# Surface flow: one wide DMA sums the K and H terms and the squares, and u is updated a slot later

## The chip, the core and the metric

The kernel runs on one core of a Trainium2 chip. The metric is the device time of one execution in microseconds (us), the median over the runs. All times are of this core. The engines are PE (TensorE, matmuls), DVE (VectorE), ACT (ScalarE), POOL (GpSimd, which here only issues DMAs that add) and SP (SyncE, which issues plain DMAs).

## What is computed

The input x is 4 x 16 images of 512 x 512 in fp32. Four layers follow each other: a window attention with an MLP (layer 0), a surface flow (layer 1), and two convolution pairs with relu (layers 2 and 3). The change lies in layer 1, which runs ten steps on each of the 64 images:

```
def step(u, _):
    ux, uy, uxx, uxy, uyy = _derivs(u)      # 3x3 Sobel filters, each result clipped to -10..10
    g2 = ux * ux + uy * uy
    denK = jnp.maximum(1.0 + g2, EPS)
    K = jnp.clip((uxx * uyy - uxy * uxy) / (denK * denK + EPS), -5.0, 5.0)
    denH = jnp.sqrt(1.0 + g2 + EPS)
    H = ((1.0 + uy * uy) * uxx - 2.0 * ux * uy * uxy + (1.0 + ux * ux) * uyy) / (2.0 * denH ** 3 + EPS)
    H = jnp.clip(H, -5.0, 5.0)
    diff = jnp.clip(alpha * K + beta * H, -1.0, 1.0)
    u = u + DT * diff
    u = jnp.pad(u[:, :, 1:-1, 1:-1], ((0, 0), (0, 0), (1, 1), (1, 1)), mode='edge')
    return (u, None)
```

## The kernel before

**Units and slots.** The surface flow holds a group of 8 images in SBUF (`surf_u`) and runs all ten steps on it, then stores it and loads the next; there are 8 groups. A group is cut into 17 units: each is 64 + 64 partitions with 2 x 512 columns, with 2 rows of halo. Group, step and unit make 8 x 10 x 17 = 1360 units, which go through a pipeline that is written out by hand: in slot `s` each engine does its share for units `s`, `s-1`, ... in a fixed order (`slot(s, par)` of each engine, called by `every_slot`). Buffers in `surf_deriv` and `surf_rest` exist twice, by the parity of the unit. `R_FIELDS` names the fields of `surf_rest` in their order in memory; each is 1024 fp32 numbers (4096 bytes) in each of 128 partitions.

**What a unit goes through.** PE makes the derivatives (L927 from u, L932 from `surf_deriv`, and the sum of the three H terms from `surf_rest`). ACT copies them from PSUM (L986, L990), squares q, p and B in one instruction (L1003), and makes 1/denK^2 and 1/denH^3 by logarithms and exponentials (L1007, L1016, L1019, L1021 give rH; L1026, L1028, L1030 give rK). DVE clips the derivatives (L1106, L1093, L1088), makes m (L1116), multiplies K together (L1124), Ha and Hc from the squares q2 and p2 (L1132), mB and nK (L1136), H (L1148), clips K and H (both on L1099), and clips their sum into `surf_ds`, scaled (L1154).

**The sums by DMA.** POOL issues DMAs that add their source to what the destination holds. In slot `s` they are, in this order: rH += rK of unit `s-4` (L1043), which is alpha K + beta H; q2 += p2 of unit `s-2` (L1049), which is g2; nK += B2 of unit `s-2` (L1054); and two that add `surf_ds` of unit `s-4` to `surf_u` (L1060), crosswise between the halves of the partitions. The waits ahead of the two sums that matter:

```
pool.wait_ge(k_clipped, s - 3)
pool.wait_ge(h_clipped, s - 3)
...
pool.wait_ge(squared, s - 1)
pool.wait_ge(hac_done, s - 1)
```

`hac_done` is told by L1132, which reads q2 and p2. DVE's L1154 waits for the sum of L1043 (`ds_sum`), ACT's L1007 for that of L1049 (`g_sum`).

**After the update.** One slot on, DVE writes the edge columns of u (L1141) and tells `updated`. SP waits for it, and exchanges halo rows between units at the end of a step (L817 to L837), or stores the group and loads the next at the end of a group (L804, L631). `unit_ready` then lets PE take the unit in its next step, 17 slots after the last one.

Of the kernel before, what the change touches and what calls it, by code (L numbers as in the profile page):

```python
# [11 lines left out]
ALU = mybir.AluOpType  # L12
# [630 lines left out]
def surface_stage(nc, x1, u10, mats, alpha_in, beta_in, STEPS, units, u, moved):  # L643
# [26 lines left out]
    with ExitStack() as ctx:  # L670
# [3 lines left out]
        def sem(name):  # L674
            return ctx.enter_context(nc.semaphore(name))
# [8 lines left out]


        D_FIELDS = ["m", "q0", "q1", "p0", "p1", "B0", "B1", "A0", "A1", "C0", "C1"]
        R_FIELDS = ["q20", "q21", "p20", "p21", "B20", "B21", "Ha0", "Ha1", "Hc0", "Hc1", "mB0", "mB1",
                    "nK0", "nK1", "rK0", "rK1", "rH0", "rH1"]
        deriv = sb("surf_deriv", [P, len(D_FIELDS), TW + 2])
        rest = sb("surf_rest", [P, len(R_FIELDS), TW])  # L690
        ds = sb("surf_ds", [P, 2, W + 4])
# [6 lines left out]
        clipped_pb, clipped_q, clipped_ac, taken_ac = sem("clipped_pb"), sem("clipped_q"), sem("clipped_ac"), sem("taken_ac")  # L698
        squared, m_done, hac_done, mbnk_done = (
            sem(n) for n in ("squared", "m_done", "hac_done", "mbnk_done"))  # L700
        g_sum, nk_sum, ds_sum, u_added = sem("g_sum"), sem("nk_sum"), sem("ds_sum"), sem("u_added")
        g_ln, g_pow, pow_ln, rh_done, den_squared, den_ln, rk_done = (
            sem(n) for n in ("g_ln", "g_pow", "pow_ln", "rh_done", "den_squared", "den_ln", "rk_done"))
        k_made, k_clipped, h_made, h_clipped, ds_clipped = (
# [3 lines left out]
        def wait(eng, s, value):  # L708

            if not isinstance(value, int) or value > 0:  # L710
                eng.wait_ge(s, value)

        def here(unit):

            return not isinstance(unit, int) or 0 <= unit < TOTAL
# [6 lines left out]
        def field(name, par=0, rows=slice(0, P), lo=0, n=TW):  # L722

            i, t, pad = place(name, par)
            return t[rows, i, pad + lo:pad + lo + n]

        def pair(a, pa, b, pb, lo=0, n=TW):

            (i, t, pad), (j, _, _) = place(a, pa), place(b, pb)
            return t[:, i:j + 1:j - i, pad + lo:pad + lo + n]  # L730

        def triple(a, b, c, par):

# [243 lines left out]
        @block.scalar  # L977
        def _(act):

            act.preload_act_table_set("natural_log_exp_and_others")  # L980

            def copy(par, phase, crossed, straight, lo=0):

                if crossed and straight:
                    n = TW - lo
                    return act.activation(pair(*crossed, *straight, lo, n), made_both(par, phase, lo, n), ACT.Copy)  # L986
                side, f = (CROSS, crossed) if crossed else (DIAG, straight)
                if lo:
                    return act.activation(field(*f, lo=lo, n=W), made_in(par, phase)[:, bank(par, phase, side, 1), :], ACT.Copy)
                return act.activation(field(*f), made_side(par, phase, side), ACT.Copy)  # L990

            def slot(s, par):

                o = 1 - par
                if here(s - 1) or here(s - 2):
                    act.wait_ge(made_ac, s)
                    wait(act, mbnk_done, s - 2)
                    copy(o, 2, ("A", o) if here(s - 1) else None, ("C", par) if here(s - 2) else None, by_dve(par)).then_inc(copied_ac, 1)
                if here(s - 2):
                    act.wait_ge(clipped_q, s - 1)  # L1000
                    act.wait_ge(clipped_pb, s)
                    wait(act, nk_sum, (s - 3) * 16)
                    act.activation(triple("q2", "p2", "B2", par), triple("q", "p", "B", par), ACT.Square).then_inc(squared, 1)  # L1003
                if here(s - 3):
                    act.wait_ge(g_sum, (s - 2) * 16)
                    wait(act, ds_clipped, s - 4)
                    act.activation(field("rH", o), field("q2", o), ACT.Ln, bias=1.0 + EPS).then_inc(g_ln, 1)  # L1007
                if here(s) or here(s - 1):
                    act.wait_ge(made_pb, s + 1)
                    if here(s - 2):  # L1010
                        wait(act, squared, s - 1)
                    wait(act, m_done, min(s - 1, TOTAL) if isinstance(s, int) else s - 1)
                    copy(par, 0, ("p", par) if here(s) else None, ("B", o) if here(s - 1) else None).then_inc(copied_pb, 1)
                if here(s - 3):
                    act.wait_ge(g_ln, s - 2)
                    act.activation(field("rH", o), field("rH", o), ACT.Exp, scale=1.5).then_inc(g_pow, 1)  # L1016
                if here(s - 3):
                    act.wait_ge(g_pow, s - 2)
                    act.activation(field("rH", o), field("rH", o), ACT.Ln, bias=EPS, scale=2.0).then_inc(pow_ln, 1)  # L1019
                    act.wait_ge(pow_ln, s - 2)  # L1020
                    act.activation(field("rH", o), field("rH", o), ACT.Exp, scale=-1.0).then_inc(rh_done, 1)  # L1021
                if here(s):
                    act.wait_ge(made_qn, s + 1)
                    copy(par, 1, ("q", par), None).then_inc(copied_q, 1)
                if here(s - 3):
                    act.activation(field("rK", o), field("q2", o), ACT.Square, bias=1.0).then_inc(den_squared, 1)  # L1026
                    act.wait_ge(den_squared, s - 2)
                    act.activation(field("rK", o), field("rK", o), ACT.Ln, bias=EPS).then_inc(den_ln, 1)  # L1028
                    act.wait_ge(den_ln, s - 2)
                    act.activation(field("rK", o), field("rK", o), ACT.Exp, scale=-1.0).then_inc(rk_done, 1)  # L1030

            every_slot(slot, act, TOTAL + 3)

        @block.gpsimd
        def _(pool):
            def slot(s, par):

                if here(s - 4):
                    pool.wait_ge(k_clipped, s - 3)
                    pool.wait_ge(h_clipped, s - 3)  # L1040
                    wait(pool, ds_sum, (s - 4) * 16)
                    pool.sem_inc(sums_begun, 1)
                    pool.dma_start(field("rH", par), field("rK", par), accum_op=ALU.add).then_inc(ds_sum, 16)  # L1043
                if here(s - 2):
                    pool.wait_ge(squared, s - 1)
                    pool.wait_ge(hac_done, s - 1)
                    wait(pool, g_sum, (s - 2) * 16)
                    pool.sem_inc(sums_begun, 1)
                    pool.dma_start(field("q2", par), field("p2", par), accum_op=ALU.add).then_inc(g_sum, 16)  # L1049
                    pool.wait_ge(mbnk_done, s - 1)  # L1050
                    pool.wait_ge(squared, s - 1)
                    wait(pool, nk_sum, (s - 2) * 16)
                    pool.sem_inc(sums_begun, 1)
                    pool.dma_start(field("nK", par), field("B2", par), accum_op=ALU.add).then_inc(nk_sum, 16)  # L1054
                if here(s - 4):
                    pool.wait_ge(ds_clipped, s - 3)
                    wait(pool, u_added, (s - 4) * 32)
                    k = bass.ds((s - 4) % UNITS, 1)
                    for found, rows in CROSSED:
                        pool.dma_start(u[rows, k, :, :].rearrange("p a t w -> p (a t w)"), flat(ds[found, :, :]),  # L1060
                                       accum_op=ALU.add).then_inc(u_added, 16)

            every_slot(slot, pool, TOTAL + 4)

        @block.vector
        def _(dve):
# [34 lines left out]
            def slot(s, par):  # L1101

                o = 1 - par
                if here(s - 2):
                    dve.wait_ge(made_ac, s)
                    dve.tensor_scalar(field("q", par), field("q", par), *CLIP).then_inc(clipped_q, 1)  # L1106
# [21 lines left out]
                if here(s - 2):  # L1128
# [6 lines left out]
                    dve.wait_ge(clipped_pb, s)  # L1135
                    dve.scalar_tensor_tensor(out=pair("mB", par, "nK", par), in0=pair("m", 0, "A", par), scalar=-1.0,  # L1136
                                             in1=pair("B", par, "C", par), op0=ALU.mult, op1=ALU.mult).then_inc(mbnk_done, 1)
                if here(s - 5):
                    dve.wait_ge(u_added, (s - 4) * 32)
                    uv = u[:, bass.ds((s - 5) % UNITS, 1), :, 2:W + 2].rearrange("p a t w -> p (a t) w")  # L1140
                    dve.tensor_scalar(uv[:, :, 0:W:W - 1], uv[:, :, 1:W - 1:W - 3], 1.0, None, ALU.mult).then_inc(updated, 1)  # L1141
                if here(s) or here(s - 1):
                    dve.wait_ge(copied_pb, s + 1)
# [1 line left out]
                if here(s - 3):  # L1145
# [3 lines left out]
                                             in1=field("rH", o), op0=ALU.mult, op1=ALU.mult).then_inc(h_made, 1)  # L1149
                    dve.wait_ge(h_made, s - 2)  # L1150
                    clip_to(field("rH", o), 1).then_inc(h_clipped, 1)
                if here(s - 4):
                    dve.wait_ge(ds_sum, (s - 3) * 16)
                    dve.tensor_scalar(ds[:, :, 2:W + 2], field("rH", par).rearrange("p (t w) -> p t w", t=2), DT, -DT,  # L1154
                                      ALU.min, ALU.max).then_inc(ds_clipped, 1)

            every_slot(slot, dve, TOTAL + 5)


PAIRS_A_GROUP = 4  # L1160
# [381 lines left out]
```

## Time and profile before

| What | Value |
|---|---|
| Median of 3 runs | 26456.31 us (26447.13 to 26471.87) |
| Profiled execution, its own time | 26429.67 us |
| Its span in the trace | 26427.9 us |
| Granted clock of TensorE, mean | 0.989 |
| PE busy | 25368.3 us (96%) |
| DVE busy | 22784.0 us (86%) |
| ACT busy | 22108.6 us (84%) |
| POOL busy | 5842.9 us (22%) |
| DMA queue of POOL (q0) | 2858.13 MB, 59.7% of 16 engines' span |

The span is that of the program's instructions on the core; the execution's own time is 2 us longer. Busy shares are means over all stages: attention up to about 5300 us, the surface flow to about 24500 us, the convolutions to the end. Only the middle one is touched. In the tables of the trace, "L1132" is line 1132 of the kernel before, an arrow names the releaser of an idle time, and `out<-in` are the program's tensors.

### The profile page before, as it was taken

The numbers are of one execution on the slowest core, as the hardware profiler recorded it, in microseconds if no ns is written. First come the engines' busy times: TensorE is split into PE (matmuls) and PEld (weight loads), VectorE is DVE, ScalarE is ACT, GpSimd is POOL, SyncE is SP. The second block draws the span as 40 slices with busy tenths as digits, with TensorE's granted clock in tenths as the row PEclk, the third lists the DMA queues.
The fourth block names the chain that finished last, engine by engine and source line by source line (L and its number), as shares of the span: only waits on it lengthen the run. The fifth ranks groups of instructions, "written<-read, shape, count | busy, mean of one in ns | idle before, by whom it ended". The sixth has DMA issues, their size and how long they took to land. (4 is left out here: it accounts for less than half of the span.)

```text
span 26427.9 us, 783402 instructions
## 1 busy us (share of the span) xinstructions
PE 25368.3 (96%) x323352; PEld 12659.5 (48%) x323352; DVE 22784.0 (86%) x22077; ACT 22108.6 (84%) x19199; POOL 5842.9 (22%) x6804
## 2 busy tenths in 40 slices
PE   8999999899999999999999999999999999999799
PEld 5666666544444443444444345434534444444465
DVE  6666666699999999999999999999999999999322
ACT  6666666699999999999999899999999998999111
POOL 0000000023323332333233233323323332333000
PEclk9999999999999999999999999999999999999899
DMA  1111111288888888888888888888888888888765
GB/s 33 32 32 32 32 32 32 44 149 156 154 171 156 154 156 170 156 155 166 159 156 154 168 155 156 158 166 156 155 167 158 156 155 167 155 156 158 120 117 101
DMA packets 1550407, 3439.19 MB, mean 130 GB/s; under 512 B 547441, under 2 KB 679153, under 8 KB 1546481
## 3 DMA queue, kind: packets, MB, share of 16 engines
q0 software_dynamic: 805120, 2858.13, 59.7%
q1 hardware_dynamic: 742512, 536.63, 10.3%
q8 instruction: 2649, 43.40, 0.7%
q14 instruction: 126, 1.02, 0.0%
HBM read 294.21 MB, written 201.33 MB: 19 GB/s over the span
## 5 line engine op out<-in xcount | busy, mean ns | idle before, releaser
L927 PE MATMUL surf_ps<-surf_u,surf_matf 64*64 64x512 f32 x87040 | 18838.6, 591 | 364.3 <-DVE surf_rest L1148 152.2
L927 PEld LDWEIGHTS surf_ps<-surf_u,surf_matf 64*64 64x64 f32 x87040 | 7290.0, 133 | 10802.3 <-issue 10547.6
L932 PE MATMUL surf_ps<-surf_deriv,surf_matf 64*64 64x512 f32 x54400 | 12051.9, 593 | 0.0
L932 PE MATMUL surf_ps<-surf_rest,surf_matf 64*64 64x512 f32 x32640 | 7237.1, 590 | 4.6 <-DVE surf_rest L1136 2.7
L1003 ACT ACTIVATE surf_rest<-surf_deriv 128x3072 f32<-128x3072 f32 x1360 | 3766.7, 2770 | 478.0 <-DVE surf_deriv L1106 394.8
L986 ACT ACTIVATE surf_deriv<-surf_ps 128x2048 f32<-128x2048 f32 (+1 forms) x2718 | 3901.0, 1435 | 258.1 <-PE surf_ps L932 251.1
L932 PEld LDWEIGHTS surf_ps<-surf_deriv,surf_matf 64*64 64x64 f32 x54400 | 3723.2, 133 | 40.8 <-issue 29.9
L1060 POOL DMA_DIRECT2D surf_u<-surf_ds x2720 | 2273.3, 973 | 4814.3 <-DVE surf_ds L1154 4314.9
L1132 DVE SCALAR_TENSOR_TENSOR surf_rest<-surf_rest,surf_deriv 128x2048 f32<-128x2048 f32 x1360 | 3106.3, 2284 | 0.3
L1136 DVE SCALAR_TENSOR_TENSOR surf_rest<-surf_deriv 128x2048 f32<-128x2048 f32 x1360 | 3106.1, 2284 | 0.0
L1049 POOL DMA_DIRECT2D surf_rest<-surf_rest x1360 | 1162.6, 855 | 7177.1 <-DVE surf_rest L1132 7166.1
L1088 DVE TENSOR_SCALAR surf_deriv<-surf_deriv 128x1024 f32<-128x1024 f32 (+1 forms) x2722 | 2597.6, 954 | 123.5 <-ACT surf_deriv L986 117.5
L1043 POOL DMA_DIRECT2D surf_rest<-surf_rest x1360 | 1218.8, 896 | 5033.6 <-DVE surf_rest L1099 5033.1
L932 PEld LDWEIGHTS surf_ps<-surf_rest,surf_matf 64*64 64x64 f32 x32640 | 2282.5, 133 | 37.3 <-issue 30.2
L1099 DVE TENSOR_SCALAR surf_rest<-surf_rest,surf_clips 128x1024 f32<-128x1024 f32 x2720 | 2209.3, 812 | 99.3
L1148 DVE SCALAR_TENSOR_TENSOR surf_rest<-surf_ps,surf_dt_ab,surf_rest 128x1024 f32<-128x1024 f32 x1360 | 1736.7, 1277 | 37.3 <-PE surf_ps L932 37.0
L1124 DVE SCALAR_TENSOR_TENSOR surf_rest<-surf_rest,surf_dt_ab 128x1024 f32<-128x1024 f32 x1360 | 1735.7, 1276 | 0.0
L407 ACT ACTIVATE att_hid<-att_w,att_b_fc 128x2048 f32<-128x2048 f32 x256 | 503.7, 1967 | 1465.0 <-PE att_w L278 1465.0
L1093 DVE TENSOR_SCALAR surf_deriv<-surf_ps 128x1024 f32<-128x1024 f32 x1359 | 1654.9, 1218 | 0.0
L1116 DVE SCALAR_TENSOR_TENSOR surf_deriv<-surf_deriv 128x1024 f32<-128x1024 f32 x1360 | 1654.7, 1217 | 0.0
L486 DVE TENSOR_REDUCE att_mx<-att_w 128x32 f32<-128x2048 f32 x512 | 1173.1, 2291 | 519.9 <-PE att_w L207 519.9
L472 DVE SCALAR_TENSOR_TENSOR att_acc<-att_xin,att_vec,att_acc 128x512 f32<-128x512 f32 x2048 | 1534.6, 749 | 54.3
(105 smaller groups left out, 31999.3 us busy)
## 6 DMA issues: line engine op xcount, KB each, us to landing
surf_rest<-surf_rest POOLq DMA_DIRECT2D x4080, 512.0 KB, 5.9
surf_u<-surf_ds POOLq DMA_DIRECT2D x2720, 258.0 KB, 5.0
att_xin<-in_x SPq DMA_DIRECT2D x2048, 41.2 KB, 2.1
attended<-att_out_rows SPq DMA_DIRECT2D x1024, 64.0 KB, 2.0
surf_u<-attended SPq DMA_DIRECT2D x512, 128.0 KB
chain_us<-flowed SPq DMA_DIRECT2D x512, 128.0 KB, 3.8
chain_xs<-attended SPq DMA_DIRECT2D x512, 128.0 KB, 4.7
out<-chain_outs SPq DMA_DIRECT2D x504, 128.0 KB, 2.8
```

Source lines behind the costliest of these rows:

```text
L927: mm = pe.matmul(dst[out, bank(par, phase, CROSS, t), :], matf[rows, mat, :], u[rows, k, t, off + 2:off + 2 + W], start=(i == 0), stop=(i ...
L932: mm = pe.matmul(dst[out, bank(par, phase, DIAG, t), :], matf[rows, mat, :], field(*fields[i], rows=rows, lo=t * W + off, n=W), start=(i = ...
L986: return act.activation(pair(*crossed, *straight, lo, n), made_both(par, phase, lo, n), ACT.Copy)
L1003: act.activation(triple("q2", "p2", "B2", par), triple("q", "p", "B", par), ACT.Square).then_inc(squared, 1)
L1060: pool.dma_start(u[rows, k, :, :].rearrange("p a t w -> p (a t w)"), flat(ds[found, :, :]), accum_op=ALU.add).then_inc(u_added, 16)
L1088: return dve.tensor_scalar(both, both, *CLIP)
L1093: return dve.tensor_scalar(pair(*first, *second, 0, W), made_both(par, phase, 0, W), *CLIP)
L1099: return dve.tensor_scalar(f, f, clips[:, which, 0:1], clips[:, which, 1:2], ALU.min, ALU.max)
L1124: dve.scalar_tensor_tensor(out=field("rK", par), in0=field("nK", par), scalar=minus_alpha, in1=field("rK", par), op0=ALU.mult, op1=ALU.mul ...
L1132: dve.scalar_tensor_tensor(out=pair("Ha", par, "Hc", par), in0=pair("q2", par, "p2", par), scalar=1.0, in1=pair("A", par, "C", par), op0=A ...
L1136: dve.scalar_tensor_tensor(out=pair("mB", par, "nK", par), in0=pair("m", 0, "A", par), scalar=-1.0, in1=pair("B", par, "C", par), op0=ALU. ...
L1148: dve.scalar_tensor_tensor(out=field("rH", o), in0=made_side(par, 1, DIAG), scalar=beta, in1=field("rH", o), op0=ALU.mult, op1=ALU.mult).t ...
```

## The change

The order of the fields in `surf_rest` is changed so that rH lies next to q2 and rK next to p2 of the same parity. One DMA with rows of 2 fields (8192 bytes) then does rH += rK of unit `s-4` and q2 += p2 of unit `s-2` at once. It waits for what either of the two waited for. The semaphores `g_sum` and `ds_sum` become one, `summed`. DVE's clip of the sum into `surf_ds`, the two DMAs that add it to u, and the edge columns are written one slot later, the first two at the start of the slot's code.

```diff
-        R_FIELDS = ["q20", "q21", "p20", "p21", "B20", "B21", "Ha0", "Ha1", "Hc0", "Hc1", "mB0", "mB1",
-                    "nK0", "nK1", "rK0", "rK1", "rH0", "rH1"]
+        R_FIELDS = ["rH0", "q20", "rK0", "p20", "Ha0", "B20", "rH1", "q21", "rK1", "p21", "Ha1", "B21",
+                    "Hc0", "Hc1", "mB0", "mB1", "nK0", "nK1"]
...
+        def run_of(a, b, par):
+
+            (i, t, pad), (j, _, _) = place(a, par), place(b, par)
+            return t[:, i:j + 1, :].rearrange("p f w -> p (f w)")
...
                 if here(s - 3):
-                    act.wait_ge(g_sum, (s - 2) * 16)
+                    act.wait_ge(summed, (s - 2) * 16)
                     wait(act, ds_clipped, s - 4)
...
-                if here(s - 4):
-                    pool.wait_ge(k_clipped, s - 3)
-                    pool.wait_ge(h_clipped, s - 3)
-                    wait(pool, ds_sum, (s - 4) * 16)
+                if here(s - 5):
+                    pool.wait_ge(ds_clipped, s - 4)
+                    wait(pool, u_added, (s - 5) * 32)
+                    k = bass.ds((s - 5) % UNITS, 1)
+                    for found, rows in CROSSED:
+                        pool.dma_start(u[rows, k, :, :].rearrange("p a t w -> p (a t w)"), flat(ds[found, :, :]),
+                                       accum_op=ALU.add).then_inc(u_added, 16)
+                if here(s - 2) or here(s - 4):
+                    if here(s - 4):
+                        pool.wait_ge(k_clipped, s - 3)
+                        pool.wait_ge(h_clipped, s - 3)
+                    if here(s - 2):
+                        pool.wait_ge(squared, s - 1)
+                        pool.wait_ge(hac_done, s - 1)
+                    wait(pool, summed, (s - 2) * 16)
                     pool.sem_inc(sums_begun, 1)
-                    pool.dma_start(field("rH", par), field("rK", par), accum_op=ALU.add).then_inc(ds_sum, 16)
+                    first, last = 0 if here(s - 4) else 1, 1 if here(s - 2) else 0
+                    pool.dma_start(run_of(("rH", "q2")[first], ("rH", "q2")[last], par),
+                                   run_of(("rK", "p2")[first], ("rK", "p2")[last], par), accum_op=ALU.add).then_inc(summed, 16)
...
+                if here(s - 5):
+                    dve.wait_ge(summed, (s - 2) * 16)
+                    wait(dve, u_added, (s - 5) * 32)
+                    dve.tensor_scalar(ds[:, :, 2:W + 2], field("rH", o).rearrange("p (t w) -> p t w", t=2), DT, -DT,
+                                      ALU.min, ALU.max).then_inc(ds_clipped, 1)
                 if here(s - 2):
                     dve.wait_ge(made_ac, s)
...
-                if here(s - 5):
-                    dve.wait_ge(u_added, (s - 4) * 32)
-                    uv = u[:, bass.ds((s - 5) % UNITS, 1), :, 2:W + 2].rearrange("p a t w -> p (a t) w")
+                if here(s - 6):
+                    dve.wait_ge(u_added, (s - 5) * 32)
+                    uv = u[:, bass.ds((s - 6) % UNITS, 1), :, 2:W + 2].rearrange("p a t w -> p (a t) w")
...
-                if here(s - 4):
-                    dve.wait_ge(ds_sum, (s - 3) * 16)
-                    dve.tensor_scalar(ds[:, :, 2:W + 2], field("rH", par).rearrange("p (t w) -> p t w", t=2), DT, -DT,
-                                      ALU.min, ALU.max).then_inc(ds_clipped, 1)
```

What stands on POOL in one slot of the loop, before. The `L711` row ahead of L1049 waits for `squared` and `hac_done`, the one ahead of L1060 for `ds_clipped`, and the one at the top for both clips, K's and H's:

```order
L711 REGISTER_ALU
L1043 DMA surf_rest<-surf_rest 128x1024
L711 REGISTER_ALU
L1049 DMA surf_rest<-surf_rest 128x1024
L1054 DMA surf_rest<-surf_rest 128x1024
L711 REGISTER_ALU
L1060 ISA
L1060 DMA surf_u<-surf_ds 64x1032
L1060 ISA
L1060 DMA surf_u<-surf_ds 64x1032
```

And after, for one slot of the same loop, where `L1048` are the additions to u, `L1060` is the wide sum and `L1067` that of nK. The `L711` row ahead of L1048 waits for `ds_clipped`, the one ahead of L1060 for `squared`, `hac_done`, `k_clipped` and `h_clipped`:

```order
L711 REGISTER_ALU
L1048 ISA
L1048 DMA surf_u<-surf_ds 64x1032
L1048 ISA
L1048 DMA surf_u<-surf_ds 64x1032
L711 REGISTER_ALU
L1060 DMA surf_rest<-surf_rest 128x2048
L1067 DMA surf_rest<-surf_rest 128x1024
```

The sum of rH and rK has moved behind `squared` and `hac_done`; the additions to u, which stood behind the nK sum of the slot before, still stand there.

DVE, before, from the second half of one slot in the loop into the next one:

```order
L1148 SCALAR_TENSOR_TENSOR surf_rest<-surf_ps,surf_dt_ab,surf_rest 128x1024
L1099 TENSOR_SCALAR surf_rest<-surf_rest,surf_clips 128x1024
L1154 TENSOR_SCALAR surf_ds<-surf_rest 128x2x512
L1106 TENSOR_SCALAR surf_deriv<-surf_deriv 128x1024
L1093 TENSOR_SCALAR surf_deriv<-surf_ps 128x2x512
L1116 SCALAR_TENSOR_TENSOR surf_deriv<-surf_deriv 128x1024
```

And after, at the same place, where L1159 answers to L1148, L1105 to L1099, L1113 to L1154, L1117 to L1106, L1099 to L1093, and L1127 to L1116:

```order
L1159 SCALAR_TENSOR_TENSOR surf_rest<-surf_ps,surf_dt_ab,surf_rest 128x1024
L1105 TENSOR_SCALAR surf_rest<-surf_rest,surf_clips 128x1024
L1111 REGISTER_ALU
L711 ISA
L1113 TENSOR_SCALAR surf_ds<-surf_rest 128x2x512
L1117 TENSOR_SCALAR surf_deriv<-surf_deriv 128x1024
L1099 TENSOR_SCALAR surf_deriv<-surf_ps 128x2x512
L1127 SCALAR_TENSOR_TENSOR surf_deriv<-surf_deriv 128x1024
```

The clip into `surf_ds` has gone from the end of one slot's code to the start of the next one's, and stands between the same two neighbours as before.

## Rows read from the trace of the kernel before

**Rows 1.** Windows: stretch, then busy us (count) of PE, PEld, DVE, ACT, POOL; clock, DMA share, GB/s.
```profile
15000.00:20000.00 5000.00, 4909.09 (x45340) 2162.54 (x45336) 4852.91 (x4600) 4759.03 (x3895) 1518.75 (x1767) 0.99 0.86 160
```

**Rows 2.** Line L1154, whole span: duration ns min/median/max, first and last start us.
```profile
L1154 DVE TENSOR_SCALAR surf_ds<-surf_rest x1360: 683/687/697, 5336.4 to 24518.4; 128x1024 f32<-128x1024 f32 x195
```

**Rows 3.** Timeline of SP's queue, 11740 to 12300 us: start, duration, line.
```profile
12008.46 0.61 SPq L825 DMA_DIRECT2D surf_u<-surf_u  x1
...
12021.31 1.27 SPq L837 DMA_DIRECT2D surf_u<-surf_u  x1
...
12242.54 0.61 SPq L825 DMA_DIRECT2D surf_u<-surf_u  x1
```

**Rows 4.** Waits, 5100 to 23900 us: total us, times, longest us.
```profile
DVE surf_u L1141 <- DMA surf_u<-surf_ds: 191.9, 95, 6.2
PE surf_ps L927 <- DVE surf_rest L1148: 140.2, 83, 4.9
PE surf_ps L927 <- SPq L898: 132.9, 8, 25.8
...
DVE surf_ds L1154 <- DMA surf_rest<-surf_rest: 31.2, 26, 3.9
```

**Rows 5.** Timeline of DVE, one undisturbed slot: start us, duration us.
```profile
12025.28 0.69 DVE L1154 TENSOR_SCALAR surf_ds<-surf_rest 128x1024 f32<-128x1024 f32 x1
...
12030.67 0.81 DVE L1099 TENSOR_SCALAR surf_rest<-surf_rest,surf_clips 128x1024 f32<-128x1024 f32 x1
12031.40 2.28 DVE L1132 SCALAR_TENSOR_TENSOR surf_rest<-surf_rest,surf_deriv 128x2048 f32<-128x2048 f32 x1
...
12037.01 1.28 DVE L1148 SCALAR_TENSOR_TENSOR surf_rest<-surf_ps,surf_dt_ab,surf_rest 128x1024 f32<-128x1024 f32 x1
...
12039.05 0.69 DVE L1154 TENSOR_SCALAR surf_ds<-surf_rest 128x1024 f32<-128x1024 f32 x1
```

**Rows 6.** Timeline of POOL, the same slot; in brackets idle before and releaser.
```profile
12026.70 1.65 POOL L1060 DMA_DIRECT2D surf_u<-surf_ds  x2 [3.13 <-DVE surf_ds L1154]
12032.16 0.90 POOL L1043 DMA_DIRECT2D surf_rest<-surf_rest  x1 [3.81 <-DVE surf_rest L1099]
12034.42 0.86 POOL L1049 DMA_DIRECT2D surf_rest<-surf_rest  x1 [1.37 <-DVE surf_rest L1132]
12036.49 0.86 POOL L1054 DMA_DIRECT2D surf_rest<-surf_rest  x1 [1.20 <-DVE surf_rest L1136]
```

**Rows 7.** Lines L1043, L1049, L1054, from 8000 to 20000 us: issue to landing.
```profile
L1043 POOL DMA_DIRECT2D surf_rest<-surf_rest x849: 892/896/922, 8004.0 to 19986.8; - x170
...
DMA to landing us min/median/max: 4.5/5.1/12.4
...
L1049 POOL DMA_DIRECT2D surf_rest<-surf_rest x849: 850/852/885, 8006.3 to 19989.0; - x170
...
DMA to landing us min/median/max: 5.1/5.6/13.4
...
L1054 POOL DMA_DIRECT2D surf_rest<-surf_rest x849: 854/857/1759, 8008.4 to 19991.1; - x170
...
DMA to landing us min/median/max: 5.8/7.0/15.9
```

**Rows 8.** DMA queues, 8000 to 20000 us: packets, MB, share of 16 engines.
```profile
q0 software_dynamic: 502756, 1784.73, 82.2%
```

**Rows 9.** Line L1043 at the end of a group, 9900 to 10235 us.
```profile
L1043 POOL DMA_DIRECT2D surf_rest<-surf_rest x20: 892/897/899, 9912.5 to 10220.7; - x20
...
DMA to landing us min/median/max: 5.0/7.6/11.0
```

**Rows 10.** Page, DMA issues: count, KB each, median us to landing.
```profile
surf_u<-surf_ds POOLq DMA_DIRECT2D x2720, 258.0 KB, 5.0
```

**Rows 11.** Timeline of ACT, the slot of rows 5.
```profile
12026.68 2.77 ACT L1003 ACTIVATE surf_rest<-surf_deriv 128x3072 f32<-128x3072 f32 x1 [0.28 <-DVE surf_deriv L1106]
...
12034.24 1.06 ACT L1021 ACTIVATE surf_rest<-surf_rest 128x1024 f32<-128x1024 f32 x1
```

More of the change, by code:

```diff
@@ L700, in surface_stage @@
             sem(n) for n in ("squared", "m_done", "hac_done", "mbnk_done"))
-        g_sum, nk_sum, ds_sum, u_added = sem("g_sum"), sem("nk_sum"), sem("ds_sum"), sem("u_added")
+        summed, nk_sum, u_added = sem("summed"), sem("nk_sum"), sem("u_added")
         g_ln, g_pow, pow_ln, rh_done, den_squared, den_ln, rk_done = (
@@ L1036, in slot @@
             def slot(s, par):
-                if here(s - 4):
-                    pool.wait_ge(k_clipped, s - 3)
-                    pool.wait_ge(h_clipped, s - 3)
-                    wait(pool, ds_sum, (s - 4) * 16)
+                if here(s - 5):
[13 more added lines that the diff above has]
+                    wait(pool, summed, (s - 2) * 16)
                     pool.sem_inc(sums_begun, 1)
-                    pool.dma_start(field("rH", par), field("rK", par), accum_op=ALU.add).then_inc(ds_sum, 16)
+                    first, last = 0 if here(s - 4) else 1, 1 if here(s - 2) else 0
+                    pool.dma_start(run_of(("rH", "q2")[first], ("rH", "q2")[last], par),
+                                   run_of(("rK", "p2")[first], ("rK", "p2")[last], par), accum_op=ALU.add).then_inc(summed, 16)
                 if here(s - 2):
[L1045 to L1049, printed above, removed]
                     pool.wait_ge(mbnk_done, s - 1)
@@ L1054, in slot @@
                     pool.dma_start(field("nK", par), field("B2", par), accum_op=ALU.add).then_inc(nk_sum, 16)
-                if here(s - 4):
[L1056 to L1063, printed above, removed]
+            every_slot(slot, pool, TOTAL + 5)
         @block.vector
@@ L1151, in slot @@
                     clip_to(field("rH", o), 1).then_inc(h_clipped, 1)
-                if here(s - 4):
-                    dve.wait_ge(ds_sum, (s - 3) * 16)
-                    dve.tensor_scalar(ds[:, :, 2:W + 2], field("rH", par).rearrange("p (t w) -> p t w", t=2), DT, -DT,
-                                      ALU.min, ALU.max).then_inc(ds_clipped, 1)
-            every_slot(slot, dve, TOTAL + 5)
+            every_slot(slot, dve, TOTAL + 6)
 PAIRS_A_GROUP = 4
```

## The prediction

> **What bounds the kernel now.** I read the windows of the surface flow first. In 5000 us of it PE is busy 4909, DVE 4853 and ACT 4759, at a granted clock of 0.99, and the DMA engines 0.86 of the time [rows 1]. PE has the least slack, and three others stand right behind it. DVE does its last clip (L1154) 1360 times between 5336.4 and 24518.4 us [rows 2]: 19182 / 1359 = 14.11 us a slot on average. The undisturbed slot is shorter: SP's first exchange transfer of a step (L825) starts at 12008.46 and again at 12242.54, 234.08 us for 17 slots, or 13.77 us [rows 3]. That is PE's own pace; the difference comes from moves at the ends of groups and a few waits. PE's named waits over the whole stage are small: 140.2 us for DVE's L1148 and 132.9 us for SP; DVE waits 191.9 us for the additions to u [rows 4]. So nothing that the change could shorten is worth more than some 1% of the time. What it could lengthen is a loop through DVE and a DMA, so the timeline of DVE and of POOL and the landing times decide.
>
> **What the change really moves.** The label says "one slot later", but the rows of the order show less. DVE's clip into ds stood last in a slot, right before the next slot's L1106 (the clip of q); now it stands first in a slot, right before that same clip of q. On POOL the additions to u likewise stand where they stood, between the nK sum and the next slot's first sum. What moved is the K+H sum: it was issued as soon as both clips were done, and is now part of a DMA that waits for DVE's L1132 too. Truly one slot later are only DVE's edge columns (L1141) and what SP does behind them.
>
> **The new loop.** Before, DVE's order in a slot is L1154, five other operations, L1099, L1132, L1136, L1141, L1088, L1148, L1099, L1154. The first L1099, the K clip, starts 12030.67 and lasts 0.81; POOL starts the sum 12032.16 (0.68 us behind its end); DVE comes to L1154 at 12039.05 [rows 5, 6]. So 6.89 us lie between issue and use, and the sum lands 5.1 us after its issue at the median and 4.5 at best [rows 7]. It is covered, and DVE waits for it hardly ever (31.2 us in all) [rows 4].
> After, the wide DMA can't be issued before L1132 has ended, since L1132 reads the squares that the DMA overwrites. From that DMA's landing the next clip into ds waits, behind it stand L1106 and all the rest of DVE's slot, up to the next L1132. That closes a loop which no buffer relaxes:
> - From the start of the clip into ds to the end of L1132: 12025.28 to 12031.40 + 2.28 = 8.40 us, back to back [rows 5].
> - From the end of L1132 to POOL's issue: 12034.42 - 12033.68 = 0.74 us [rows 5, 6].
> - From issue to landing of 1024 KB, call it L.
> - From landing to DVE's start: I take none.
>
> The slot is the larger of 13.77 and 9.14 + L. PE stays the bound only if L is at most 4.6 us.
>
> **The price L.** No row shows a DMA of 1024 KB. Two ways lead to it from the rows of 512 KB. First, L1043 lands at best 4.5 us after issue; L1049 is issued 2.26 us behind it (12034.42 - 12032.16) and lands at best 5.1 after issue, so 2.26 + 5.1 - 4.5 = 2.9 us behind it: that is what a second 512 KB costs a queue that is already running [rows 6, 7]. Second, in the 12000 us from 8000 the accumulating queue takes 82.2% of the engines for 1784.73 MB [rows 8]; 0.524 MB then takes 0.524 / 1784.73 x 0.822 x 12000 = 2.9 us of all 16. All rows of that queue are of 4096 or 4128 bytes; no row gives the time of one of 8192, so that bytes are cheaper in wide rows stays a rival. The sum: L = 4.5 + 2.9 = 7.4 at best and 5.1 + 2.9 = 8.0 at the median. One DMA has one fixed part less than two, but that part (4.5 - 2.9 = 1.6 us) was hidden in parallel before, and is in series now.
> The Trainium skill, "DMA: Bandwidth & Descriptors", on the anatomy of one DMA, gives about 2.0 us plus bytes over 436 GB/s, and its rules advise to batch to 1 MiB: by that a second 512 KB adds 1.2 us, L would be 6.3 and the slot 15.4, which is slower too. The rows of this trace show 2.9 us for it, and the sum goes by them.
>
> **The sum.** Undisturbed slot: 9.14 + 8.0 = 17.14 us. At the end of a group SP stores and loads images for some 335 us, and there L1043 lands after 7.6 us at the median, not 5.1 [rows 9]; twice the bytes would meet twice the excess of 2.5, or 5.0; SP also waits between its own batches, and of the 5.0 I take 3.5, so L = 11.5 and the slot 20.7. (With none of it or all of it the total moves by 400 down or 100 up.) Seven such stretches hold 7 x 335 / 20.7 = 113 slots. Stage: 1247 x 17.14 + 113 x 20.7 = 21374 + 2339 = 23713 us. Before it was 19182. The rest of the program (attention ahead, convolutions behind) is not touched; one more drain slot is some 10 us. Profiled execution: span 26427.9, own time 26429.67; plus 4531 plus 10 is 30970. The median of the runs is 27 us above that execution, 0.1%, so I say 31000.
>
> **What else moves, and why I cost it at nothing.** POOL issues three DMAs instead of four plus the same two additions, saving 0.89 us of an engine that has over 9 us idle in a slot [rows 6]. The additions to u are issued at the slot's start, 7 us ahead of the wide DMA, and land in 5.0 us at the median [rows 10], so they aren't in its way. ACT: the squares (L1003) start 1.40 us after the clip into ds (12026.68 - 12025.28) and last 2.77, so they end 2 us before L1132 starts; rh is done (L1021) at 12035.30, before L1148 at 12037.01 [rows 5, 11]. ACT's logarithm needs the same DMA that DVE has by then waited for. The nK sum is used two slots on. The edge columns one slot later: SP's exchange takes 12008.46 to 12022.58 plus a landing [rows 3], and the units it frees are needed more than three slots after the old place of L1141, more than two (over 34 us) after the new one. At a group's end PE waits for SP 132.9 us in all [rows 4]; SP's chain there is made of its own transfers and gets hardly longer, while 17 slots now last 57 us more, so this wait should go. It lies inside the 19182 that I replace.
>
> **Rivals.**
> - Rows of 8192 bytes are cheap, the second half costs 1.2 us or so as the fixed part dominates: slot 9.14 + 6.3 = 15.44, stage 21000, time 28300. For it: one DMA less to complete; against it: both working-outs at 2.9 us. 6%.
> - Rows are free (a packet costs the same at either size): L = 5.1, slot 14.24; stage 19370 plus the groups' ends, say 26900. 2%.
> - The other side: L at most 4.6 us, PE stays the bound, and the waits of DVE for u (191.9) and of PE for L1148 (140.2) go [rows 4]: about 26250. It needs a megabyte to land as fast as the fastest half megabyte. 2%.
> - Worse than forecast: the exchange that L1141 releases starts about 1.6 us after the wide DMA's issue and shares its engines. The nK sum stands at that place now, and lands at 7.0 with 5.8 at best, 1.2 above [rows 7]. With L 1.2 higher in each slot: + 1630, 32600. Or PE, which would now stand idle some 3.4 us in 17, is granted less clock. 8%.
>
> **How the numbers follow.** The forecast has 82%. Its own range: L = 7.4 everywhere gives 16.54 x 1360 = 22494, time 29750; L = 8.9 gives about 32200. I give 29300 to 32200, which leaves out the first three rivals and half of the fourth. Some 0.2% (50 us) is what this measurement can tell from no change; slower by more has 0.96, within it 0.02, faster 0.02.
>
> **What would show it.** DVE's clip into ds waits for "DMA surf_rest<-surf_rest" in nearly each of 1360 slots, about 3.4 us (17.14 - 13.77, plus DVE's old slack of some 0.3), 4700 us in all. The wide DMA lands at a median of 8.0 us. SP's first exchange returns after 291 us, not 234. DVE, ACT and PE fall to about 0.8 of the window, PE waits for DVE's L1148, and the DMA share falls to about 0.7. Wrong if the wide DMA lands much under 7.4, or if ds is clipped without a wait.

## The result, and the profile after

The change makes the kernel slower: 30638.47 us median (30621.95 to 30649.31, 4 runs) against 26459.26 us (26447.13 to 26471.87, 4 runs). The ratio is 1.1579, with a 95% interval of 1.1559 to 1.1599. Forecast was 31000 with 29300 to 32200. The profiled execution took 30633.81 us, its span 30632.0 us; 4204 us more than before's.

The page of the kernel after: busy time by engine, the group of DVE's clip into `surf_ds` (L1113 now; the number behind the last bar is the idle time ahead of it), and the issues of POOL with their KB and median us to landing.

```profile
PE 26643.0 (87%) x323352; PEld 12086.8 (39%) x323352; DVE 22883.3 (75%) x22077; ACT 22162.2 (72%) x19199; POOL 4655.6 (15%) x5446
...
L1113 DVE TENSOR_SCALAR surf_ds<-surf_rest 128x1024 f32<-128x1024 f32 x1360 | 945.9, 696 | 4544.6 <-DMA surf_rest<-surf_rest 4544.5
...
surf_rest<-surf_rest POOLq DMA_DIRECT2D x1358, 1024.0 KB, 7.1
surf_u<-surf_ds POOLq DMA_DIRECT2D x2720, 258.0 KB, 5.0
surf_rest<-surf_rest POOLq DMA_DIRECT2D x1364, 512.0 KB, 8.5
```

DVE does the same work as before (22883 us against 22784), but waits 4544.5 us in one place, where it waited 31.2 [rows 4]. The window that answers to [rows 1]:

```profile
15000.00:20000.00 5000.00, 4300.17 (x37232) 1664.47 (x37224) 4007.19 (x3776) 3917.70 (x3199) 994.49 (x1162) 0.95 0.69 131
```

The row has the same columns as [rows 1]. No engine is full any more, and neither are the DMA engines (0.69, was 0.86). If nobody is full, look for a circle of waits. The waits of the stage (5300 to 28800 us) name its members:

```profile
POOL surf_rest L1060 <- DVE surf_rest L1143: 13488.8, 1344, 5307.1
POOL surf_u L1048 <- DVE surf_ds L1113: 8731.5, 1346, 12.2
DVE surf_ds L1113 <- DMA surf_rest<-surf_rest: 4544.5, 1358, 11.6
ACT surf_rest L1008 <- DVE surf_deriv L1117: 4236.0, 1319, 9.2
PE surf_ps L932 <- issue: 3091.8, 1298, 8.3
```

POOL waits for DVE's L1143 (L1132 before), DVE waits for the DMA that POOL then issues, ACT waits for DVE behind it, and PE, which was the bound, stands idle 3092 us. PE's wait for SP is gone from the list, and DVE's for the additions to u is down to 5.7 us.

The timeline of DVE, three slots on end; from each L1113 to the next is a slot, and L1143 is what POOL waits for.

```profile
15028.59 0.70 DVE L1113 TENSOR_SCALAR surf_ds<-surf_rest 128x1024 f32<-128x1024 f32 x1 [2.48 <-DMA surf_rest<-surf_rest]
...
15044.99 0.69 DVE L1113 TENSOR_SCALAR surf_ds<-surf_rest 128x1024 f32<-128x1024 f32 x1 [2.54 <-DMA surf_rest<-surf_rest]
...
15051.12 2.29 DVE L1143 SCALAR_TENSOR_TENSOR surf_rest<-surf_rest,surf_deriv 128x2048 f32<-128x2048 f32 x1
...
15061.33 0.69 DVE L1113 TENSOR_SCALAR surf_ds<-surf_rest 128x1024 f32<-128x1024 f32 x1 [2.47 <-DMA surf_rest<-surf_rest]
...
15071.85 0.17 DVE L1152 TENSOR_SCALAR surf_u<-surf_u  x1
...
15079.91 0.70 DVE L1113 TENSOR_SCALAR surf_ds<-surf_rest 128x1024 f32<-128x1024 f32 x1 [4.71 <-DMA surf_rest<-surf_rest]
...
15081.11 1.22 DVE L1099 TENSOR_SCALAR surf_deriv<-surf_ps 128x1024 f32<-128x1024 f32 x1
```

And POOL's issues of the wide DMA in the last two of them, and three of SP's L830, the transfer that begins an exchange (L825 before). The first and the last are a step apart, and the second is the next exchange of the same step; a step has four.

```profile
15054.15 0.89 POOL L1060 DMA_DIRECT2D surf_rest<-surf_rest  x1 [6.07 <-DVE surf_rest L1143]
...
15070.56 0.89 POOL L1060 DMA_DIRECT2D surf_rest<-surf_rest  x1 [6.13 <-DVE surf_rest L1143]
```

```profile
15004.41 0.61 SPq L830 DMA_DIRECT2D surf_u<-surf_u  x1
...
15072.05 0.62 SPq L830 DMA_DIRECT2D surf_u<-surf_u  x1
...
15291.93 0.61 SPq L830 DMA_DIRECT2D surf_u<-surf_u  x1
```

The loop can be read off in one slot. DVE's L1113 starts 15044.99; L1143 ends at 15051.12 + 2.29 = 15053.41, which is 8.42 us on. POOL issues 0.74 us later. From 15054.15 to DVE's next L1113 at 15061.33 are 7.18 us. The sum is 16.34 us, where a slot took 13.77 before [rows 3]; undisturbed slots last 16.34 or 16.40 us, by turns, 16.37 on average. The next slot takes 18.58: in it the edge columns (L1152, 15071.85) let SP's exchange go at 15072.05, just 1.5 us behind the wide DMA (15070.56), and DVE waits 4.71 us, not 2.5. SP's period of 17 slots is 15291.93 - 15004.41 = 287.52 us (234.08 before), and over the whole stage:

```profile
L1113 DVE TENSOR_SCALAR surf_ds<-surf_rest x1360: 687/695/700, 5343.9 to 28721.7; 128x1024 f32<-128x1024 f32 x195
...
L1060 POOL DMA_DIRECT2D surf_rest<-surf_rest x1362: 857/892/1279, 5307.5 to 28710.6; - x195
...
DMA to landing us min/median/max: 5.0/7.1/13.5
```

The last start less the first is 23378 us, and 23378 / 1359 = 17.20 us a slot, where [rows 2] gave 14.11. The stage grew by 4196 us: nearly all of the 4204.

The page puts PE's idle time to "issue", that is, to nothing that it can name. The timeline names it. In the slot that begins at 15079.91 PE starts again at 15082.44:

```profile
15082.44 1.12 PE L932 MATMUL surf_ps<-surf_u,surf_matf 64*64 64x512 f32 x2 [4.17 <-issue]
```

That is 0.11 us behind the end of DVE's L1099 (15081.11 + 1.22 = 15082.33), which takes derivatives from PSUM; the code has PE wait for it (`taken_ac`) before it writes there again. Of the 3110 us in idle stretches of PE above 0.3 us in this stage, 3027 us end less than 0.16 us behind an L1099. So PE stands behind DVE, and DVE behind the wide DMA.

### The profile page after: what moved, and what is told of

It is laid out like the page before. It is cut to its first block and busy times, and to the rows that moved or that the text cites. A ratio compares the mean times of both kernels' runs of the same rounds, so it can differ in the third digit from the quotient of the medians.

```text
span 30632.0 us, 780694 instructions
## 1 busy us (share of the span) xinstructions
PE 26643.0 (87%) x323352; PEld 12086.8 (39%) x323352; DVE 22883.3 (75%) x22077; ACT 22162.2 (72%) x19199; POOL 4655.6 (15%) x5446
## 5 line engine op out<-in xcount | busy, mean ns | idle before, releaser
L932 PE MATMUL surf_ps<-surf_u,surf_matf 64*64 64x512 f32 x87040 | 20085.7, 614 | 3278.5 <-issue 3091.8
L932 PEld LDWEIGHTS surf_ps<-surf_u,surf_matf 64*64 64x64 f32 x87040 | 7213.9, 137 | 15623.2 <-issue 15622.2
L937 PE MATMUL surf_ps<-surf_rest,surf_matf 64*64 64x512 f32 x32640 | 8206.1, 654 | 5.8 <-DVE surf_deriv L1101 5.2
L1113 DVE TENSOR_SCALAR surf_ds<-surf_rest 128x1024 f32<-128x1024 f32 x1360 | 945.9, 696 | 4544.6 <-DMA surf_rest<-surf_rest 4544.5
L1048 POOL DMA_DIRECT2D surf_u<-surf_ds x2720 | 2266.7, 980 | 8845.6 <-DVE surf_ds L1113 8731.5
L1060 POOL DMA_DIRECT2D surf_rest<-surf_rest x1362 | 1222.7, 898 | 13609.9 <-DVE surf_rest L1143 13488.8
L1147 DVE SCALAR_TENSOR_TENSOR surf_rest<-surf_deriv 128x2048 f32<-128x2048 f32 x1360 | 3108.1, 2285 | 0.0
L1143 DVE SCALAR_TENSOR_TENSOR surf_rest<-surf_rest,surf_deriv 128x2048 f32<-128x2048 f32 x1360 | 3107.8, 2285 | 0.3
L937 PEld LDWEIGHTS surf_ps<-surf_rest,surf_matf 64*64 64x64 f32 x32640 | 2375.3, 146 | 18.3 <-issue 18.3
L1105 DVE TENSOR_SCALAR surf_rest<-surf_rest,surf_clips 128x1024 f32<-128x1024 f32 x2720 | 2210.6, 813 | 99.6
L1159 DVE SCALAR_TENSOR_TENSOR surf_rest<-surf_ps,surf_dt_ab,surf_rest 128x1024 f32<-128x1024 f32 x1360 | 1738.9, 1279 | 9.1 <-PE surf_ps L937 6.3
L1127 DVE SCALAR_TENSOR_TENSOR surf_deriv<-surf_deriv 128x1024 f32<-128x1024 f32 x1360 | 1656.7, 1218 | 0.0
L1099 DVE TENSOR_SCALAR surf_deriv<-surf_ps 128x1024 f32<-128x1024 f32 x1359 | 1656.4, 1219 | 0.0
```

What stands on the lines that cost most here:

```text
L932: mm = pe.matmul(dst[out, bank(par, phase, CROSS, t), :], matf[rows, mat, :], u[rows, k, t, off + 2:off + 2 + W], start=(i == 0), stop=(i ...
L937: mm = pe.matmul(dst[out, bank(par, phase, DIAG, t), :], matf[rows, mat, :], field(*fields[i], rows=rows, lo=t * W + off, n=W), start=(i = ...
L1105: return dve.tensor_scalar(f, f, clips[:, which, 0:1], clips[:, which, 1:2], ALU.min, ALU.max)
L1127: dve.scalar_tensor_tensor(out=field("m"), in0=field("q", par), scalar=2.0, in1=field("p", par), op0=ALU.mult, op1=ALU.mult).then_inc(m_do ...
L1143: dve.scalar_tensor_tensor(out=pair("Ha", par, "Hc", par), in0=pair("q2", par, "p2", par), scalar=1.0, in1=pair("A", par, "C", par), op0=A ...
L1159: dve.scalar_tensor_tensor(out=field("rH", o), in0=made_side(par, 1, DIAG), scalar=beta, in1=field("rH", o), op0=ALU.mult, op1=ALU.mult).t ...
```

## The experiments

All times are medians, and each ratio is to the kernel before on the same chip. Where a kernel is compared with the kernel after, that is across chips, on which the kernel before took 26459 to 26481 us.

**Two DMAs again, the rest of the change kept.**

```diff
+                if here(s - 4):
+                    pool.wait_ge(k_clipped, s - 3)
+                    pool.wait_ge(h_clipped, s - 3)
+                    wait(pool, ds_sum, (s - 4) * 16)
+                    pool.sem_inc(sums_begun, 1)
+                    pool.dma_start(field("rH", par), field("rK", par), accum_op=ALU.add).then_inc(ds_sum, 16)
+                if here(s - 2):
+                    pool.wait_ge(squared, s - 1)
+                    pool.wait_ge(hac_done, s - 1)
...
-                    dve.wait_ge(summed, (s - 2) * 16)
+                    dve.wait_ge(ds_sum, (s - 4) * 16)
```

> The kernel after, with the wide DMA taken apart into two of 512 KB: rH += rK goes out as soon as both clips are done, q2 += p2 after L1132's counterpart, each with its own semaphore; fields, order of DVE and the update one slot later stay. If the loop from the wide DMA's landing over DVE's clip into ds to its next issue is the cause, DVE's wait ahead of that clip falls from 4544 us to under 100 and the time is that of before, 26250 to 26500; a little less than 26459 if the waits of the edge columns for the additions to u (227 us) go as well. If the later update, or the new order of fields, is the cause, the time stays near 30640.

Measured: 26501.37 us against 26461.26, ratio 1.001 (1.0 to 1.0019). The 4180 us are gone: the wide DMA made them, not the update a slot later. DVE's wait ahead of the clip fell from 4544 to 231 us, not to under 100, and the time came out just above the expected range: the hope of a small gain failed. DVE's wait for the additions to u went (7.3 us), but PE now waits longer for SP at the ends of groups, since SP gets its units a slot later. PE's waits in this kernel:

```profile
PE surf_ps L932 <- SPq L903: 227.1, 13, 28.1
```

Before it was 132.9 us in 8 waits [rows 4].

**The wide DMA alone, all else in its old slot.** It is the kernel before with the new order of fields, `run_of` and the wide DMA of the diff above; DVE keeps its code, with `dve.wait_ge(summed, (s - 1) * 16)` ahead of the clip.

> The kernel before with the new order of fields and the wide DMA, but the clip into ds, the additions to u and the edge columns in the slot where they stood (the nK sum now guarded as in the kernel after). The clip into ds keeps its neighbours on DVE either way, so the loop through the wide DMA is the same: 30640, give or take 200. If the delay of the update by a slot were what costs, it would be near 26460.

Measured: 30469.99 us, ratio 1.151 (1.1492 to 1.1528). The other half of the proof: the wide DMA without the later update costs 4000 us. (In this kernel the nK sum keeps the guard `here(s - 2)` of the kernel after; without it POOL waits at the end for a unit that does not exist, and the kernel never ends.) That it is 170 us below the kernel after is within the 200 that were allowed, but it has a place. DVE's timeline and POOL's in this kernel show where it lies:

```profile
15042.12 0.69 DVE L1160 TENSOR_SCALAR surf_ds<-surf_rest 128x1024 f32<-128x1024 f32 x1 [2.35 <-DMA surf_rest<-surf_rest]
...
15093.51 0.69 DVE L1160 TENSOR_SCALAR surf_ds<-surf_rest 128x1024 f32<-128x1024 f32 x1 [2.36 <-DMA surf_rest<-surf_rest]
...
15109.72 0.69 DVE L1160 TENSOR_SCALAR surf_ds<-surf_rest 128x1024 f32<-128x1024 f32 x1 [2.34 <-DMA surf_rest<-surf_rest]
```

```profile
15035.05 0.89 POOL L1053 DMA_DIRECT2D surf_rest<-surf_rest  x1 [6.06 <-DVE surf_rest L1138]
...
15102.66 0.89 POOL L1053 DMA_DIRECT2D surf_rest<-surf_rest  x1 [6.05 <-DVE surf_rest L1138]
```

Its slot is 16.21 us (15093.51 to 15109.72), and from issue to DVE's clip are 7.06 to 7.07 us, where the kernel after has 7.18. The landing times in the two traces show 7.05 us from issue to landing in undisturbed slots of both, and then 0.12 us from landing to clip in the kernel after, 0.02 in this one. In the kernel after two waits stand ahead of the clip (`summed`, then `u_added`), in this one a single wait. The others go the same way: 0.02 us in the kernel before, which also has one wait, and 0.12 to 0.14 in after_edges_first, wide_rows_4096 and split_late_issue, which have two (ds_before_m, with two, has 0.12 or 0.23). So the second wait fits as the cause of some 0.1 us a slot, 140 of the 170 us, but it was not tried alone.

**The order of fields alone.** R_FIELDS as in the diff, nothing else.

> The kernel before with the new order of fields in surf_rest and nothing else. If memory layout plays no part: 26460 within 30 us. If it does (rows of DVE's and ACT's operands at other distances), the durations of L1132, L1136 and L1003 change and the time with them.

Measured: 26475.84 us, ratio 0.9998 (0.9989 to 1.0007). Layout plays no part; L1132 takes 2285 ns, as before (2284).

**More cover for the DMA: the clip into ds further back on DVE.** In two doses, from the kernel after: the block goes from the start of the slot to a place ahead of the instruction that makes m (ds_before_m), or, unchanged, right behind that instruction (ds_after_m).

```diff
-                if here(s - 5):
-                    dve.wait_ge(summed, (s - 2) * 16)
-                    wait(dve, u_added, (s - 5) * 32)
-                    dve.tensor_scalar(ds[:, :, 2:W + 2], field("rH", o).rearrange("p (t w) -> p t w", t=2), DT, -DT,
-                                      ALU.min, ALU.max).then_inc(ds_clipped, 1)
                 if here(s - 2):
                     dve.wait_ge(made_ac, s)
...
+                if here(s - 5):
+                    dve.wait_ge(summed, (s - 2) * 16)
+                    wait(dve, u_added, (s - 5) * 32)
+                    dve.tensor_scalar(ds[:, :, 2:W + 2], field("rH", o).rearrange("p (t w) -> p t w", t=2), DT, -DT,
+                                      ALU.min, ALU.max).then_inc(ds_clipped, 1)
                 if here(s - 2):
                     dve.wait_ge(clipped_q, s - 1)
                     dve.wait_ge(clipped_pb, s - 1)
```

> The kernel after with the clip into ds moved back by two DVE operations, behind the clip of q and the take from PSUM (0.60 + 1.13 us), so that the DMA has 1.73 us more cover in each slot. Loop: 1360 x 1.73 = 2350 us less than 30638, so 28290. If instead the DMA queue as such is too slow for a slot (contention), or the clock of TensorE is the cause, moving the clip changes little: over 30000.

> The same with the clip one operation further back, behind m: 2.87 us more cover than after. The loop is 16.2 - 2.87 = 13.3 us in undisturbed slots, under the 13.77 of TensorE, so these are as fast as before; slots whose wide DMA lands 2 us late (about a third) still lose some 1.6 us, 0.3 x 1360 x 1.6 = 650: 26600 to 27300. By the rival (contention as such): over 30000.

Measured: 28428.97 us (1.0742, 1.0724 to 1.076) and 27113.48 us (1.0245, 1.0228 to 1.0262). The first dose gives back 2210 / 1360 = 1.6 us a slot for 1.73 us of cover, the second 0.97 more for 1.13, as PE's pace comes near. If the queue as such were too slow, this could not be: all of these kernels move the same bytes. DVE's row of the first:

```profile
15035.82 0.70 DVE L1122 TENSOR_SCALAR surf_ds<-surf_rest 128x1024 f32<-128x1024 f32 x1 [0.73 <-DMA surf_rest<-surf_rest]
```

Its wait of 2.5 us has become 0.73, less by just about the 1.73 us that the clip was moved. The second is still 650 us above the kernel before; m_edges_first below shows what most of that is.

**Late issue without double size.** The kernel split_later with one line more ahead of the sum of K and H; the sum of the squares is issued right behind it.

```diff
+                    wait(pool, hac_done, min(s - 1, TOTAL) if isinstance(s, int) else s - 1)
                     wait(pool, ds_sum, (s - 4) * 16)
```

> The kernel split_later with one more wait: POOL issues the sum of the K and H terms only when L1132's counterpart has ended, as the wide DMA had to, and the sum of the squares right behind it. So the late issue is there, but the clip into ds waits for 512 KB alone (4.5 us at best, 5.4 on average). Loop: 9.14 + 4.6 = 13.74 us at best, just what TensorE takes; landings above that are no longer covered, up to 0.9 us a slot on average: 26700 to 27500. If the late issue alone made the kernel after slow, it would be near 30600; if only the size did, at 26501.

Measured: 27382.19 us, ratio 1.0346 (1.0329 to 1.0364). The late issue by itself costs 920 us over the kernel before (880 over split_later, which differs by the one line), and the second half megabyte in the same DMA takes it to 4180. The waits of this kernel:

```profile
DVE surf_ds L1114 <- DMA surf_rest<-surf_rest: 1036.6, 501, 13.7
```

The wait is there in 501 slots, not in all: its loop is near PE's pace, and mostly the late landings show. Not all of the 920 us need be that wait: ACT's logarithm (L1012) here waits 563 us for the sum of the squares, which is issued later too, where it waited 15.5 us in the kernel before.

**One DMA, rows of 4096 bytes.** The kernel after with the old order of fields, so that rH and q2 lie apart and the one DMA moves two runs a partition.

```diff
-            (i, t, pad), (j, _, _) = place(a, par), place(b, par)
-            return t[:, i:j + 1, :].rearrange("p f w -> p (f w)")
+            if a == b:
+                return field(a, par)
+            return pair(b, par, a, par)
```

> The kernel after, with one DMA for both sums still, but with the old order of fields, so that its rows are two pieces of 4096 bytes that lie apart. Theory: the wide DMA landed 7.1 us after issue where two halves in a row gave 4.5 + 2.9 = 7.4; if the rows of 8192 bytes saved the 0.3 us, this one lands at 7.4 and the time is 1360 x 0.3 = 400 us more, 31040. Rival: the width of rows has no effect and the 0.3 us was a start that two DMAs pay each; then it lands at 7.1 and the time stays 30640. Either way it is far from 26460, since the loop doesn't depend on rows.

Measured: 32331.17 us, ratio 1.2212 (1.2193 to 1.2231), a miss by 1300 us: whether a partition has one run of 8192 bytes or two of 4096 that lie apart matters far more than I had thought. (Width and distance change together here; that the order of fields alone costs nothing was measured with DMAs of 512 KB.) Line L1061 in this kernel, 8000 to 20000 us:

```profile
L1061 POOL DMA_DIRECT2D surf_rest<-surf_rest x650: 1217/1217/2053, 8014.3 to 19996.7; - x163
...
DMA to landing us min/median/max: 7.9/8.0/14.3
```

The issue takes 1.22 us, not 0.89, and the landing 8.0, not 7.1; the 0.9 us are counted from the start of the issue, so the longer issue may be a third of them. 0.9 us a slot is 1220 us of the 1690. The rest is mostly in slots that SP's transfers disturb. Here is one with an exchange, from one clip into ds to the next:

```profile
15060.11 0.70 DVE L1114 TENSOR_SCALAR surf_ds<-surf_rest 128x1024 f32<-128x1024 f32 x1 [3.43 <-DMA surf_rest<-surf_rest]
15081.33 0.69 DVE L1114 TENSOR_SCALAR surf_ds<-surf_rest 128x1024 f32<-128x1024 f32 x1 [7.34 <-DMA surf_rest<-surf_rest]
```

It lasts 21.22 us where the one in the kernel after lasted 18.58.

**SP's exchange out of the wide DMA's way.** The edge columns on DVE right behind the clip into ds; what they wait for has landed by then.

```diff
                                       ALU.min, ALU.max).then_inc(ds_clipped, 1)
+                if here(s - 6):
+                    dve.wait_ge(u_added, (s - 5) * 32)
+                    uv = u[:, bass.ds((s - 6) % UNITS, 1), :, 2:W + 2].rearrange("p a t w -> p (a t) w")
+                    dve.tensor_scalar(uv[:, :, 0:W:W - 1], uv[:, :, 1:W - 1:W - 3], 1.0, None, ALU.mult).then_inc(updated, 1)
...
```

> The kernel after with one move: DVE's edge columns right behind the clip into ds instead of behind L1147, 9 us earlier in the slot. In the kernel after, the wide DMA lands 7.05 us after issue in most slots but at 9.2 in those where SP's exchange, which the edge columns release 1.3 us after the wide DMA's issue, is under way. Theory: the exchange's first big rows collide with the wide DMA; released 9 us earlier they are through by then: some 300 slots lose 2.1 us less, 30638 - 630 = 30000. Rival: SP's ten moves last 14 us and hit a wide DMA wherever they start: 30500 to 30700.

Measured: 30025.65 us, ratio 1.135 (1.1332 to 1.1367): 613 us less from one instruction of 0.17 us moved, as expected. DVE's wait for the wide DMA:

```profile
DVE surf_ds L1113 <- DMA surf_rest<-surf_rest: 3944.3, 1360, 8.5
```

It is 600 us less. Four exchanges a step, nine steps of ten, eight groups are 288 slots; 613 / 288 = 2.1 us each. That is a little too low: the edge columns now stand inside the loop and make its undisturbed slot longer, 16.44 us instead of 16.37. The same move in the kernel with the clip behind m (there the edge columns come first in the slot):

> The kernel with the clip into ds behind m (27113), and the edge columns first in DVE's slot. Theory: what is left over the kernel before, 650 us, is late landings of the wide DMA (DVE waits 892 us for it), of which the exchange causes the greater part: 26500 to 26750. Rival: the 1039 us that ACT's logarithm waits for the clip into ds, which overwrites what it reads, are what is left: 27000 and over.

Measured: 26614.32 us, ratio 1.0063 (1.0048 to 1.0079). 500 of the 650 us that were left go; with cover and with the exchange out of the way the wide DMA is nearly free, but not better than two DMAs.

**A version under both.** Two DMAs, and the edge columns first:

> The kernel split_later (two DMAs of 512 KB, update a slot later, 26501) with the edge columns right behind the clip into ds: their additions have landed long before, so DVE never waits for them, and SP starts only 3.9 us later than in the kernel before instead of 13.8. If the 227 us that TensorE waits for SP in split_later come from the delay, they fall towards 133, and the time to 26300 to 26430, under both kernels. If nothing comes of it, 26460 to 26500.

Measured: 26423.58 us against 26460.37, ratio 0.9988 (0.9979 to 0.9997), the lowest median of all, 37 us under the kernel before. PE's wait for SP:

```profile
PE surf_ps L932 <- SPq L903: 148.5, 7, 29.5
```

The other way, aimed at the same gain, the edge columns of the kernel before moved behind the clip of H, was

> The kernel before with one move: the edge columns behind the clip of H, still in the same slot, 3.3 us later on DVE. If the 227 us that DVE waits there for the additions to u hold up its multiplication of H and then TensorE, these go, and SP starts only 3 us later instead of a slot: 26300 to 26430. If that wait is slack that TensorE's pace hides, no change: 26460. If SP's chain at the ends of groups counts, a few us more.

Measured: 26454.51 us against 26481.15, ratio 0.999 (0.9981 to 0.9999). Both gains are of 0.1%, at the edge of what the runs resolve, and less than hoped; that either kernel is truly faster than the one before is not shown.

## Why the prediction was right

- **What moved.** That the clip into ds keeps its neighbours on DVE and that the sum of K and H is what moves was the key. The two runs that took the change apart bear it out: wide DMA alone 30470, later update alone 26501.
- **The fixed part of the loop.** Forecast 8.40 + 0.74 us; measured 8.42 + 0.74. Right. That DVE would start at once on landing was off by 0.12 us a slot.
- **L, the landing of 1024 KB.** Forecast 8.0 at the median and 7.4 at best; measured 7.1 and, in the undisturbed slots, 7.0. This term was mis-sized, by two things. The second half costs 7.0 - 4.5 = 2.5 us in rows of 8192 bytes, not 2.9. (With rows of 4096 bytes it costs more than 2.9: the DMA lands after 7.9 us at best where the forecast had 7.4. That its median is the forecast 8.0 is luck, two errors of opposite sign.) And I carried over the 0.6 us between best and median of L1043; in the kernel after best and median are 0.1 apart (7.0 and 7.1). I take that 0.6 for traffic of the faster kernel, which is not shown. The rival that rows of 8192 bytes are cheap had a little of the truth: 0.9 us of landing, not the 1.7 that it needed.
- **The disturbed slots.** Forecast: 113 slots at the groups' ends at 20.7 us, which adds 113 x 3.56 = 400 us, and nothing for the exchanges. Measured: 23378 - 1359 x 16.37 = 1130 us over the undisturbed pace, of which the exchange's collision with the wide DMA is at least 613, by experiment. So the exchanges are the term that was wrongly put at nothing. I had named the collision among the worse cases (1.2 us in each slot); it is 2.1 us in one slot of five. The groups' ends cost less than forecast. At one of them:

```profile
L1060 POOL DMA_DIRECT2D surf_rest<-surf_rest x16: 892/895/1274, 13900.7 to 14182.7; - x16
...
DMA to landing us min/median/max: 7.3/8.6/13.1
```

The forecast had 11.5 us there and slots of 20.7; DVE's 14 slots from 13891.50 to 14153.47 us last 18.7 on average, which makes some 270 us for all seven stretches.
- **How near the sum came.** 17.44 us a slot were forecast and 17.20 measured. That is nearer than its terms deserve, and luck: L was 0.9 us too high in every slot, which is some 1200 us too much, and the landing to clip and the disturbed slots were some 900 too low.
- **What else moves.** POOL, ACT and the additions to u cost nothing, as said. PE's wait for SP at the groups' ends vanished, as said, because the slots became longer; at the old pace (split_later) the same delay makes it grow from 133 to 227 us. DVE's wait was forecast at 4700 us and was 4544.5 (the terms beside that forecast, 3.37 + 0.3 us a slot, make 4990, not 4700); SP's period at 291 us and was 287.5.
- **PE.** The idle time is there (3092 us), but not where it was forecast. PE waits only 171 us for L1159, the H multiplication (L1148 before); nearly all the rest ends with DVE's L1099, the take from PSUM behind the late clip.

## What to carry to other kernels

Before merging two transfers, list what each waited for and who waits for each. The merged one is issued with the later of the two and lands later than either half (here 7.0 us behind its issue, where half of it took 4.5), and if the earlier half fed an instruction that stands ahead of the later half's releaser on an in-order engine, a loop closes whose length is to be compared with the bound's pace. A transfer on such a loop wants cover of its whole landing time in the order of the engine that waits; here each us of cover was worth nearly a us a slot up to the bound's pace. What an instruction releases on another queue (here an exchange of halo rows) should be placed so that it does not start right behind such a transfer.

## What the runs showed of the hardware that I had not expected

- An accumulating DMA of 1024 KB lands in 7.0 to 7.1 us with 128 rows of 8192 bytes and in 8.0 with 256 runs of 4096; its issue on POOL takes 0.89 us against 1.22.
- A DMA issued at once behind another takes longer to issue: in split_late_issue the second (L1062) takes 2.05 us on POOL at the median, where L1049 took 0.85. The first (L1056) takes 0.90 as ever.

```profile
L1062 POOL DMA_DIRECT2D surf_rest<-surf_rest x1360: 852/2048/2212, 5305.6 to 25416.8; - x195
```

- The granted clock in the window shown was 0.95 on average, where it was 0.99 before. It is at 2.4 GHz (1.00) most of the time and falls to 1.2 GHz (0.50) for short stretches, as right here, where PE had just stood idle for 4.17 us:

```profile
15082.50:15085.00 2.50, 2.50 (x12) 0.79 (x16) 2.50 (x3) 2.50 (x3) 0.50 (x1) 0.50 0.96 164
```

It set nothing here, since no one in the loop waits for PE: in the whole stage DVE waits for it 25 us (18.9 ahead of L1117 and 6.3 ahead of L1159).
